# Finer runs in the edge sort of a graph-attention kernel: rows of 32 with runs of 8, masks in descending order, a layer norm shared by two engines

## The chip, the cores and the metric

The kernel runs on one core of one Trainium2 chip. The metric is the device time of one execution in microseconds (us). Every kernel is executed several times, and profiled once by the hardware profiler. A 0.3% difference, about 7 us, is what a measurement of this kernel can tell from none.

## The reference

The input is a graph with N = 6250 nodes of width D = 256 and E = 100000 edges (`src`, `dst`). Cut to what matters:

```python
xn = _layernorm(x)
x = x + gnn(xn, W_w, W_b, a_w, a_b, src, dst) + mix(xn)
x = x + ffn(_layernorm(x))
# gnn: Wh = xn @ W_w + W_b; e = leaky(f_dst[dst] + f_src[src] + a_b)
#      softmax of e over the edges of each src node, then the weighted sum of Wh[dst], relu
# mix: linear attention (phi(q), phi(k), 8 heads) @ Wo + bo, residual, layer norm 1 (l1g, l1b),
#      relu(. @ W1 + b1) @ W2 + b2, residual, layer norm 2
# ffn: mixture of 6 experts, two per node, three layers each
```

## The kernel before, in words

The program is a sequence of blocks with a barrier between them; inside a block five engines run hand-ordered instruction lists that meet at semaphores.

**Block 1** (L450 to L1243) makes the node table `wh_table`, sorts the edges by their source block, and does the attention half of `mix`. There are NT = 50 node blocks of R = 125 rows. The 100000 edges lie on 128 partitions as KC = 28 chunks of W = 28 columns each.

*The first pass* (until about 300 us) counts: for each block ScalarE makes a mask, VectorE scans it. From the counts VectorE works out (L681 to L698) where each run, that is the edges of one chunk and partition that belong to one block, begins. Runs are padded to LO = 64 places.

*The second pass* (L755 to L766, 50 steps b = 0 to 49) gives each edge its place: a mask "block is b" lets `copy_predicated` (L764) write the base of block b's run into `bpos`. For even b the mask comes from ScalarE in two instructions, Abs (L935) and Relu (L939); for odd b VectorE makes it itself with `is_equal` (L761).

*The address part* (L771 to L864) turns places into a row `hih` and a column `loh` of a small matrix of HI = 106 rows by LO = 64 columns per chunk, and works out where each row goes in DRAM (`dest`, L793 to L797: a compare-and-multiply and a reduction over 1400 elements).

*The compaction* (L893 to L909 on VectorE, 28 chunks k) places the edges of one chunk into their matrix by one-hot matmuls. Per chunk VectorE makes the one-hot rows (`first_half`, L873), the one-hot columns (`low_half`, L876) and two payloads (`payload`, L879 and L880); TensorE multiplies them (`compact`, L1206, 28 matmuls); ScalarE copies a half (L1068); `join` (L888) puts the two halves together in `stage`, of which there are three. GpSimd then writes the matrix to DRAM in one indirect DMA per chunk (L532): one address per row, 64 elements behind it. It waits for the write of the chunk before to have landed (L531), because a later chunk's run overwrites the padding of an earlier one; `join` waits for the write three chunks back (L887). When all have landed, SP reads the sorted slots back (L482), they are transposed and become the index and row tables, and block 1 ends.

*The attention of `mix`* is threaded through all of this after the first pass: 25 chunks of 250 nodes, a new one every SLOT = 6 slots, each with steps at fixed slot offsets on PE, ACT and DVE (the four functions `attend`). A slot is one step of the second pass, then one of TAB_SLOTS places in the address part, then a quarter of a compaction chunk. The steps that matter here are `attend_sum` at offset 13 (DVE: residual, bias, `bn_stats`, `bn_aggr`), `root` at 14 (ACT), and `attend_norm` at 15, where VectorE applies layer norm 1 in two passes of two instructions (`norm_out`, L293 and L299). SP stores the result `x1` to DRAM (L471).

**Block 2** (L1305 to L1694) is the graph attention. GpSimd gathers the table rows of the edges, 812 indirect DMAs of 128 rows (L1330). The other engines go over NG = 251 groups of four tiles in a software pipeline (`together`, L100): a group is at `turn` at lag 1 and `fetch` at lag 3 on PE, at `total` at lag 6 (L1648) and at `gather_up` at lag 7 on DVE (L1438). The feed-forward half of `mix` is threaded in, one of the 25 chunks every PER = 10 slots: 250 slots, then TAIL = 8 slots in which the last groups drain. In slot 1 ScalarE copies the turned input `x1T` out of PSUM (`feed_in`, L1577). Layer norm 2 of a chunk (`feed_sum` L1446, bias, moments L1457, totals, centre L1470, scale, out L1485) is done by VectorE in slots 0 to 5 of the next ten.

**Blocks 3 and 4** route the nodes to experts (with indirect writes of 128 rows of 1056 bytes, L1839) and run the experts (with accumulating indirect writes of 128 rows of 1024 bytes, L2139). The diff does not touch them.

Of the kernel before, what the change touches and what calls it, by code (L numbers as in the profile page):

```python
# [14 lines left out]
I32 = mybir.dt.int32  # L15
# [38 lines left out]
SPARE = 940  # L54
SLOT, TAB_SLOTS = 6, 8
# [12 lines left out]
TAIL = NG - PER * NC + LAG  # L68
assert L == 2 ** 7 and TILES - GT >= MOST and NB - RING <= NG <= 2 * L and 3 <= TAIL <= PER and NT * R == N and NC * 2 == NT

# [57 lines left out]
def gps_kernel(nc, x, src, dst, gW, gWb, ga, gab, Wq, bq, Wk, bk, Wv, bv, Wo, bo, W1, b1, W2, b2,  # L128
# [6 lines left out]
    with ExitStack() as ctx:  # L135
# [60 lines left out]
        rs = take(2, 2)  # L196
        pair_rows = take.place[0]
# [49 lines left out]
        dest = take(KC).bitcast(I32)  # L247
        dsum, dcol = take(KC), take(KC)
        icol, i64 = take(1), take(1)
# [5 lines left out]
        prod = E_  # L255
# [11 lines left out]
        held_gpsimd = sem("held_gpsimd")  # L267

        def hold(eng):

            eng.sem_inc(held_gpsimd if eng is nc.gpsimd else held_vector, 1)

        def norm_in(dve, c, k, bias):

            mine = m_ln[k]
            dve.wait_ge(mine, at(c, 4, 1))
            nc.vector.tensor_tensor(y1[0:R, k, :, :], y1[0:R, k, :, :], bias[0:R, :].unsqueeze(1).to_broadcast([R, 2, D]), ALU.add).then_inc(mine, 1)
            dve.wait_ge(mine, at(c, 4, 2))
            for r in range(2):
                last_s = nc.vector.bn_stats(stats[0:R, k, r, :], y1[0:R, k, r, :])  # L280
            last_s.then_inc(mine, 1)
            dve.wait_ge(mine, at(c, 4, 3))
            hold(dve)
            for r in range(2):
                last_s = nc.vector.bn_aggr(mv[0:R, k, r, :], stats[0:R, k, r, :])
            last_s.then_inc(m_va[k], 1)

        def norm_out(dve, c, k, dst_of, gam, bet):

            mine = m_ln[k]  # L290
            dve.wait_ge(m_va[k], at(c, 1, 1))
            for r in range(2):
                last_s = nc.vector.scalar_tensor_tensor(y1[0:R, k, r, :], y1[0:R, k, r, :], mv[0:R, k, r, 0:1], gam[0:R, :],  # L293
                                                ALU.subtract, ALU.mult)
            last_s.then_inc(mine, 1)
            dve.wait_ge(mine, at(c, 4, 4))
# [2044 lines left out]
```

## Time and profile before

| | us |
|---|---|
| runs, unprofiled | 2337.33, 2339.25, 2344.64 |
| their median | 2339.25 |
| the profiled execution, own time | 2334.28 |
| its span, first to last instruction | 2332.6 |
| second pass | 327.3 to 436.4 |
| address part | 436.4 to 475 |
| compaction, to the last write's landing | 475 to 741 |
| block 2 | from about 749 to 1820.5 |
| blocks 3 and 4 | 1820.5 to 2332.6 |

In the rows below times are us from the span's start unless marked ns, and L12 is line 12 of the kernel. PE is TensorE's matmul, PEld its weight load, DVE VectorE, ACT ScalarE, POOL GpSimd, SP SyncE. A busy PE is modelled and not PE at its peak; spans on POOL are rough, and end when the instruction is done, not when its data has landed. "Releaser" is what an engine's idle time ended with.

### The profile page before, as it was taken

How to read it: one execution, taken by the hardware profiler on the slowest of the kernel's cores; microseconds unless marked ns; L12 is line 12 of the kernel's file. 1: busy time of each engine (PE TensorE's matmuls, PEld its weight loads, DVE VectorE, ACT ScalarE, POOL GpSimd, SP SyncE). 2: the span in 40 equal slices, each digit the busy share in tenths (PEclk: the TensorE clock that was granted, in tenths of full speed). 3: DMA queues.
4: the chain of work that ended last, by engine and by line, in shares of the span. 5: the costliest groups of instructions: out<-in, count | busy, mean ns of one | idle time of the engine just before them, and what ended most of it. 6: DMA issues, size and time to landing. Idle time of an engine off the chain costs nothing. (4 is left out here: it accounts for less than half of the span.)

```text
span 2332.6 us, 50389 instructions
## 1 busy us (share of the span) xinstructions
PE 1929.0 (83%) x10277; PEld 1565.8 (67%) x10277; DVE 1757.9 (75%) x5456; ACT 1446.1 (62%) x4447; POOL 1106.9 (47%) x1090
## 2 busy tenths in 40 slices
PE   2888856678884799999999999999999563699996
PEld 1444435467773587787877877778787463588885
DVE  7877769989995688888888888888888652254553
ACT  4666647423330588888988889898898661233332
POOL 1000000001113777777777767777775267255554
PEclk9999978779995799999999999999999765799999
DMA  4200000011111444444444434444443543255553
GB/s 139 65 24 28 27 7 19 14 55 22 22 22 37 118 118 122 118 123 118 122 119 118 123 109 113 118 116 123 115 121 86 163 162 133 63 89 96 92 95 56
DMA packets 115204, 205.88 MB, mean 88 GB/s; under 512 B 27026, under 2 KB 69387, under 8 KB 114907
## 3 DMA queue, kind: packets, MB, share of 16 engines
q0 software_dynamic: 61648, 135.33, 24.2%
q1 hardware_dynamic: 48601, 59.88, 8.5%
q10 hardware_dynamic: 4658, 7.46, 1.1%
q8 instruction: 96, 1.57, 0.3%
q14 instruction: 201, 1.65, 0.2%
HBM read 146.67 MB, written 50.02 MB: 84 GB/s over the span
## 5 line engine op out<-in xcount | busy, mean ns | idle before, releaser
L1330 POOL DMA_INDIRECT area<-wh_table,area x812 | 782.5, 964 | 269.5 <-issue 241.7
L1648 PE MATMUL bank<-area 128*126 x2008 | 495.9, 389 | 35.1 <-ACT area L1564 15.7
L1648 PEld LDWEIGHTS bank<-area 128*126 128x126 f32 x2008 | 357.6, 188 | 110.3 <-issue 59.5
L1363 DVE TENSOR_SCALAR area<-iota_row,area 128x126 f32<-128x126 f32 x1004 | 359.7, 366 | 22.2 <-ACT area L1524 18.2
L1557 ACT ACTIVATE area<-iota_row,area 128x126 f32<-128x126 f32 x753 | 292.2, 389 | 0.4 <-ACT area L1564 0.3
L2139 POOL DMA_INDIRECT out_dram<-area x108 | 169.5, 1570 | 165.2 <-DVE area L2200 148.5
L1571 ACT ACTIVATE area<-area 128x126 f32<-128x126 f32 x753 | 243.1, 386 | 0.5
L527 POOL IOTA acc_mem<- 50x812 f32 x1 | 0.8, 807 | 450.0 <-DVE area L797 450.0
L1438 DVE SCALAR_TENSOR_TENSOR acc_mem<-acc_mem,area,bank 125x258 f32 x251 | 120.4, 480 | 110.6 <-PE bank L1636 97.6
L1510 ACT ACTIVATE area<-bank 125x512 bf16<-125x512 f32 x251 | 149.3, 595 | 85.9 <-DVE area L1377 83.6
L1668 PE MATMUL bank<-area 128*128 128x250 f32 x800 | 190.4, 381 | 5.9 <-ACT area L1577 3.1
L1624 PE MATMUL bank<-ident,area 128*126 128x128 f32 x1004 | 161.3, 284 | 35.5 <-DVE area L1363 34.7
L1679 PE MATMUL bank<-area 128*125 128x256 f32 x800 | 189.0, 379 | 0.0
L1668 PEld LDWEIGHTS bank<-area 128*128 128x128 f32 x800 | 154.3, 193 | 26.2 <-ACT area L1577 3.5
L1377 DVE TENSOR_REDUCE area<-bank 125x1 f32<-125x512 f32 x251 | 171.3, 682 | 0.0
L1679 PEld LDWEIGHTS bank<-area 128*125 128x125 f32 x800 | 150.1, 188 | 22.9
L532 POOL DMA_INDIRECT sorted_slots<-area x28 | 45.9, 1641 | 234.2 <-DVE area L888 213.3
L2200 DVE SCALAR_TENSOR_TENSOR area<-bank,area 128x256 f32<-128x256 f32 x108 | 47.3, 479 | 143.4 <-DMA out_dram<-area 78.0
L1624 PEld LDWEIGHTS bank<-ident,area 128*126 128x126 f32 x1004 | 106.3, 141 | 40.4 <-DVE area L1363 39.7
L2232 ACT ACTIVATE area<-bank,area 128x256 f32<-128x256 f32 x108 | 45.3, 471 | 141.6 <-issue 133.6
L1839 POOL DMA_INDIRECT moe_rows<-area x100 | 99.3, 993 | 66.6 <-ACT area L1989 36.7
L1206 PE MATMUL bank<-area 128*128 128x128 f16 x784 | 104.6, 298 | 7.5 <-DVE area L888 7.5
(409 smaller groups left out, 4188.8 us busy)
## 6 DMA issues: line engine op xcount, KB each, us to landing
area<-moe_rows SPq DMA_DIRECT2D x54, 264.0 KB, 2.7
area<-wh_table,area POOLq DMA_INDIRECT x812
area<-area SPq DMA_DIRECT2D x18, 388.5 KB
wh_table<-area SPq DMA_DIRECT2D x50, 126.5 KB
xn<-in_x_dram SPq DMA_DIRECT2D x25, 250.0 KB
x_rows<-area SPq DMA_DIRECT2D x25, 250.0 KB
area<-x_rows ACTq DMA_DIRECT2D x24, 250.0 KB
area<-in_L_ffn_expert_w_dram SPq DMA_DIRECT2D x3, 1536.0 KB, 11.8
```

The source lines that it names most:

```text
L1330: g.indirect_dma_start(out=gath[:, (i + GT) % RS, :], out_offset=None, in_=table, in_offset=bass.IndirectOffsetOnAxis(ap=idx_tab[:, i:i + ...
L1363: ins = V.tensor_scalar(xm[:, b, t, :], iota_row[:, :], rowl[:, j % 10, t:t + 1], fetched(j, D)[:, t:t + 1], ALU.is_equal, ALU.mult)
L1377: V.tensor_reduce(gmax[0:R, b:b + 1], bank[XT[j % 2]][0:R, :], AX.X, ALU.max).then_inc(d_m, 1)
L1438: V.scalar_tensor_tensor(row, row, alpha[0:R, j % 5:j % 5 + 1], bank[US[b]][0:R, 0:WROW], ALU.mult, ALU.add).then_inc(d_acc, 1)
L1510: A.activation(hot[0:R, b, :], bank[XT[j % 2]][0:R, :], ACT.Sign).then_inc(a_hot, 1)
L1557: last = A.activation(dist[:, t, :], iota_row[:, :], ACT.Abs, bias=rowl[:, j % 10, t:t + 1], scale=-1.0)
L1571: last = A.activation(sm[:, b, t, :], dist[:, t, :], ACT.Exp, bias=e3[:, b, t:t + 1], scale=-1.0e12)
L1624: last = T.transpose(bank[XT[j % 2]][0:RW, t * L:(t + 1) * L], xm[:, b, t, :], ident[:, :])
L1648: last = T.matmul(bank[US[b]][0:RW, 0:WROW], sm[:, b, t, :], gath[:, bass.ds(place + t, 1), 0:WROW].rearrange("p a w -> p (a w)"), start=( ...
L1668: last = T.matmul(bank[HB[p % 2]][:, i * CH:(i + 1) * CH], w_1[:, k, f * 128:(f + 1) * 128], x1T[:, k, :], start=(k == 0), stop=(k == 1))
L1679: last = T.matmul(bank[AB][0:R, r * D:(r + 1) * D], hT[:, f, r * R:(r + 1) * R], w_2[:, f, :], start=(f == 0), stop=(f == 7))
L2139: g.indirect_dma_start(out=out, out_offset=bass.IndirectOffsetOnAxis(ap=rowi[:, j % RB6, s, MW - 2:MW - 1], axis=0), in_=yo[:, j % 3, s, : ...
```

## The change

- Rows of the compaction matrix get LO = 32 columns in place of 64, and runs are padded to RUN = 8 places in place of 64. HI goes from 106 to 123 rows of the matrix, and the write uses all 128 partitions. A row now holds RL = 4 runs, and each goes to an address of its own.
- The indirect write of a chunk becomes four, one for each run of a row: 128 addresses with 8 elements (32 bytes) each. They are issued without a wait between them; the wait for the chunk before stays. The addresses are worked out four times, once for each run of a row.
- Less padding makes 788 tiles in place of 812, and 245 groups (NG) in place of 251. TAIL becomes 6.
- The second pass goes downward, b = 49 to 0. Its mask is "block is at most b", one Relu on ScalarE for every b; what is written wrongly is overwritten later. VectorE's own masks and the Abs are gone. There are four mask buffers in turn.
- Layer norm 1: VectorE works out minus mean times root on a [125, 2] tile (offset 15), ScalarE applies scale and shift in two activations (`normal`, offset 16), VectorE multiplies by the gain in one instruction (offset 17). The shift `l1b` is added by ScalarE when it copies `x1T` out of PSUM (two instructions in place of one), and once to `bias_2`. TAB_SLOTS becomes 10.

The diff, cut to its core:

```diff
-LO, LO_BITS = 64, 6
-HI = (L * W + NT * (LO - 1)) // LO + 1
+LO, LO_BITS = 32, 5
+RUN, RUN_BITS = 8, 3
+RL = LO // RUN
+HI = (L * W + NT * (RUN - 1)) // LO + 1
-MOST = (E + NT * (LO - 1) + L - 1) // L
+MOST = (E + NT * (RUN - 1) + L - 1) // L
-SLOT, TAB_SLOTS = 6, 8
+SLOT, TAB_SLOTS = 6, 10
-TAIL = NG - PER * NC + LAG
+TAIL = max(6, NG - PER * NC + LAG)
...
                     if k > 0:
-                        g.wait_ge(sent_runs, 16 * k)
-                    g.indirect_dma_start(out=slots.rearrange("(a b) -> a b", b=1),
-                                         out_offset=bass.IndirectOffsetOnAxis(ap=dest[0:HI, k:k + 1], axis=0),
-                                         in_=stage[0:HI, k % 3, :], in_offset=None).then_inc(sent_runs, 16)
+                        g.wait_ge(sent_runs, 16 * RL * k)
+                    for j in range(RL):
+                        g.indirect_dma_start(out=slots.rearrange("(a b) -> a b", b=1),
+                                             out_offset=bass.IndirectOffsetOnAxis(ap=dest[:, j, k:k + 1], axis=0),
+                                             in_=stage[:, k % 3, j * RUN:(j + 1) * RUN], in_offset=None).then_inc(sent_runs, 16)
...
+                V.tensor_tensor(bias_2, bias_2, be1, ALU.add)
...
+                def attend_gain(c, j):
+                    dve.wait_ge(m_n, at(c, 1, 1))
+                    V.tensor_tensor(x1[0:R, j, :, :], x1[0:R, j, :, :], g1[0:R, :].unsqueeze(1).to_broadcast([R, 2, D]), ALU.mult).then_inc(m_x1, 1)
...
-                def attend_norm(c, j):
-                    if at(c) >= 2:
-                        dve.wait_ge(rows_moved[j], 16 * SG + at(c, 8, -8 * j))
-                    norm_out(dve, c, 0, x1[0:R, j, :, :], g1, be1).then_inc(m_x1, 1)
+                def attend_norm(c):
...
+                    V.scalar_tensor_tensor(nmu[0:R, :], mv[0:R, 0, :, 0], -1.0, rs[0:R, 0, :], ALU.mult, ALU.mult).then_inc(m_va[0], 1)
...
-                for b in range(NT):
-                    if b % 2 == 0:
-                        dve.wait_ge(mask_ready, NT + b // 2 + 1)
-                        m = masks[(b // 2) % 2]
-                    else:
-                        m = masks[2 + (b // 2) % 2]
-                        step(V.tensor_scalar(m, blk, float(b), None, ALU.is_equal))
-                    if b > 0:
-                        dve.wait_ge(placed, NT + b)
+                for i in range(NT):
+                    b, m = NT - 1 - i, masks[i % 4]
+                    dve.wait_ge(mask_ready, NT + i + 1)
+                    if i > 0:
+                        dve.wait_ge(placed, NT + i)
...
-                step(V.scalar_tensor_tensor(E_[:, 0:KC, :], pin, icol, delta[:, 0:KC, :], ALU.is_le, ALU.mult))
-                step(V.tensor_reduce(dsum, E_[:, 0:KC, :], AX.X, ALU.add))
-                attend(NT + 6)
-                step(V.tensor_tensor(dcol, dsum, D_[:, :, 0:1].rearrange("p k b -> p (k b)"), ALU.add))
-                V.tensor_scalar(dest, dcol, i64, None, ALU.add).then_inc(dest_ready, 1)
+                for i in range(RL):
+                    step(V.scalar_tensor_tensor(over_runs, pin, icol[:, i:i + 1], delta[:, 0:KC, :], ALU.is_le, ALU.mult))
+                    step(V.tensor_reduce(dsum[:, i, :], over_runs, AX.X, ALU.add))
+                    attend(NT + 6 + i)
+                    step(V.tensor_tensor(dcol[:, i, :], dsum[:, i, :], first, ALU.add))
+                    last_d = V.tensor_scalar(dest[:, i, :], dcol[:, i, :], irun[:, i:i + 1], None, ALU.add)
...
+                def normal(c, j):
+                    act.wait_ge(m_va[0], at(c, 2, 2))
+                    if at(c) >= 2:
+                        act.wait_ge(rows_moved[j], 16 * SG + at(c, 8, -8 * j))
+                    for r in range(2):
+                        last = A.activation(x1[0:R, j, r, :], y1[0:R, 0, r, :], ACT.Identity, bias=nmu[0:R, r:r + 1], scale=rs[0:R, 0, r:r + 1])
+                    last.then_inc(m_n, 1)
...
+                def at_most(i):
+
+                    b = NT - 1 - i
+                    act.wait_ge(placed, NT + max(0, i - 3))
+                    A.activation(masks[i % 4], blk, ACT.Relu, bias=iota_blk[:, b + 1:b + 2], scale=-1.0).then_inc(mask_ready, 1)
...
-                    A.copy(x1T, bank[TB][:, 0:2 * CH].rearrange("p (k n) -> p k n", k=2)).then_inc(m_tc1, 1)
+                    for k in range(2):
+                        last = A.activation(x1T[:, k, :], bank[TB][:, k * CH:(k + 1) * CH], ACT.Identity, bias=be1_col[:, k:k + 1])
+                    last.then_inc(m_tc1, 1)
```

## Rows read from the trace of the kernel before

**Rows 1.** The head of the page.
```profile
span 2332.6 us, 50389 instructions
```

**Rows 2.** Busy time per stage: PE, PEld, DVE, ACT, POOL, PEclk, DMA share, GB/s.
```profile
327.30:436.40 109.10, 72.60 (x308) 60.11 (x308) 98.81 (x170) 79.74 (x134) 0.00 (x0) 0.76 0.05 15
436.40:475.00 38.60, 19.45 (x68) 13.49 (x68) 35.70 (x97) 9.07 (x22) 0.81 (x1) 0.64 0.05 14
503.40:715.00 211.60, 182.22 (x1219) 160.52 (x1218) 196.94 (x328) 67.15 (x178) 36.02 (x23) 0.96 0.14 33
757.70:1798.20 1040.50, 969.66 (x5632) 811.75 (x5633) 888.92 (x3481) 899.04 (x3226) 776.51 (x806) 0.99 0.43 118
1798.20:1820.50 22.30, 15.85 (x85) 11.51 (x83) 16.03 (x58) 17.20 (x62) 0.00 (x0) 1.00 0.01 1
```

**Rows 3.** Groups by line, second pass (327.3 to 436.4): count, busy us, mean ns, idle.
```profile
L935 ACT ACTIVATE acc_mem<-acc_mem,iota_blk 128x784 f32<-128x784 f32 x25 | 23.7, 949 | 14.4 <-issue 14.4
...
L761 DVE TENSOR_SCALAR acc_mem<-acc_mem 128x784 f32<-128x784 f32 x25 | 13.6, 544 | 0.0
...
L1006 ACT ACTIVATE area<-xn,area 125x256 f32<-125x256 f32 x18 | 9.7, 589 | 0.0
```

**Rows 4.** Timeline of DVE in the address part: start, duration.
```profile
452.94 1.64 DVE L793 SCALAR_TENSOR_TENSOR area<-area 128x1400 f32<-128x1400 f32 x1
454.62 1.61 DVE L794 TENSOR_REDUCE area<-area 128x28 f32<-128x1400 f32 x1
```

**Rows 5.** Groups by line, compaction from 503.4 to 715.
```profile
L873 DVE TENSOR_TENSOR area<-acc_mem 128x2968 f16<-128x2968 f16 x24 | 40.8, 1701 | 6.3 <-PE bank L1206 5.5
...
L876 DVE TENSOR_TENSOR area<-acc_mem,area 128x1792 f16<-128x1792 f16 x23 | 24.6, 1068 | 0.0
...
L299 DVE SCALAR_TENSOR_TENSOR area<-area 125x256 f32<-125x256 f32 x32 | 14.1, 482 | 0.6
...
L277 DVE TENSOR_TENSOR area<-area 125x512 f32<-125x512 f32 x15 | 10.4, 692 | 0.5
```

**Rows 6.** Timeline of POOL at the end of the compaction.
```profile
726.81 1.54 POOL L532 DMA_INDIRECT sorted_slots<-area  x1 [2.97 <-DMA sorted_slots<-area]
731.70 1.55 POOL L532 DMA_INDIRECT sorted_slots<-area  x1 [3.35 <-DMA sorted_slots<-area]
```

**Rows 7.** Line L532, the indirect write of the compaction: ns min/median/max, landing.
```profile
L532 POOL DMA_INDIRECT sorted_slots<-area x28: 1543/1547/3729, 503.8 to 736.6; - x28
...
DMA to landing us min/median/max: 3.6/4.1/8.9
```

**Rows 8.** Line L1839, the indirect write of block 3.
```profile
L1839 POOL DMA_INDIRECT moe_rows<-area x100: 965/970/1507, 1849.3 to 1988.6; - x100
...
DMA to landing us min/median/max: 2.4/2.6/4.7
```

**Rows 9.** Line L2139, the accumulating indirect write of block 4.
```profile
L2139 POOL DMA_INDIRECT out_dram<-area x108: 1542/1551/1783, 2024.4 to 2322.8; - x108
```

**Rows 10.** Timeline of POOL in block 3: two writes in a row.
```profile
1855.11 0.97 POOL L1839 DMA_INDIRECT moe_rows<-area  x1 [0.30 <-issue]
1856.38 0.97 POOL L1839 DMA_INDIRECT moe_rows<-area  x1 [0.30 <-issue]
```

**Rows 11.** DMA view, 721 to 727, which holds the packets of one indirect write.
```profile
DMA packets 80, 0.03 MB, mean 5 GB/s; under 512 B 72, under 2 KB 74, under 8 KB 80
...
sorted_slots<-area POOLq DMA_INDIRECT x2, 3.8
```

**Rows 12.** Timeline of DVE in the tail of block 2.
```profile
1801.91 0.69 DVE L1446 TENSOR_TENSOR area<-bank,area 125x512 f32<-125x512 f32 x1
...
1808.77 0.75 DVE L1457 BATCH_NORM_STATS2 area<-area 125x6 f32<-125x256 f32 x2
...
1811.45 0.87 DVE L1470 SCALAR_TENSOR_TENSOR area<-area 125x256 f32<-125x256 f32 x2
...
1820.02 0.48 DVE L1438 SCALAR_TENSOR_TENSOR acc_mem<-acc_mem,area,bank 125x258 f32 x1 [1.60 <-PE bank L1648]
```

**Rows 13.** Line L1577, the copy of x1T: ns min/median/max.
```profile
L1577 ACT COPY area<-bank x25: 548/552/556, 766.9 to 1765.5; 128x500 f32<-128x500 f32 x25
...
  PE bank L1668: 3.1, 1
```

More of the change, by code:

```diff
@@ L196, in gps_kernel @@
         rs = take(2, 2)
+        nmu = take(2)
+        be1_col = take(2)
         pair_rows = take.place[0]
@@ L266, in gps_kernel @@
         held_vector = sem("held_vector")
-        held_gpsimd = sem("held_gpsimd")
         def hold(eng):
[L271 to L278, printed above, removed]
+            eng.sem_inc(held_vector, 1)
@@ L283, in norm_in @@
             hold(dve)
             for r in range(2):
[L285 to L296, printed above, removed]
-            dve.wait_ge(m_rs[k], at(c, 1, 1))
-            for r in range(2):
-                last_s = nc.vector.scalar_tensor_tensor(dst_of[:, r, :], y1[0:R, k, r, :], rs[0:R, k, r:r + 1], bet[0:R, :],
-                                                ALU.mult, ALU.add)
-            return last_s
+                last_s = nc.vector.bn_aggr(mv[0:R, 0, r, :], stats[0:R, 0, r, :])
@@ L778, in _ @@
                 cnt = Sv[:, KC, :]
-                step(V.tensor_scalar(ntf, cnt, float(LO - 1), None, ALU.add))
+                step(V.tensor_scalar(ntf, cnt, float(RUN - 1), None, ALU.add))
                 attend(NT + 1)
@@ L800, in _ @@
                 V.tensor_copy(int50, tend)
-                step(V.tensor_scalar(end50, tend, float(L - LO), None, ALU.add))
+                step(V.tensor_scalar(end50, tend, float(L - RUN), None, ALU.add))
                 V.tensor_scalar(int50, int50, 7, None, ALU.logical_shift_right)
@@ L1002, in prepare @@
                     m = at(c) % 3
-                    wait(act, m_ln[0], at(c, 4, -11))
+                    wait(act, m_ln[0], at(c, 3, -8))
                     for r in range(2):
@@ L1031, in inverses @@
                     A.copy(rec_row[0:R, :, :, :], rec8[0:R, :, :].unsqueeze(3).to_broadcast([R, 2, 8, HD])).then_inc(m_inv, 1)
+                def normal(c, j):
[5 more added lines that the diff above has]
+                    last.then_inc(m_n, 1)
                 def attend(slot):
+                    c = chunk_at(slot, 16)
+                    if c is not None:
+                        normal(c, at(c) % 2)
                     c = chunk_at(slot, 14)
@@ L1067, in _ @@
                             act.wait_ge(staged, k - 3)
[L1068 removed]
+                        A.copy(half[:, k % 2, :], bank[KV + k % 2][:, LO:2 * LO]).then_inc(halved, 1)
                     for i in range(4):
@@ L1173, in o @@
                     pe.wait_ge(m_att, at(c, 1, 1))
-                    wait(pe, m_ln[0], at(c, 4, -3))
+                    wait(pe, m_ln[0], at(c, 3, -2))
                     for r in range(2):
```

82 lines of the change are left out of this document (47 added, 35 removed).

## The prediction, made before the changed kernel ran

> **What bounds the kernel now.** I first read the span [rows 1] and the chain of waits. The chain covers only the last 300 us (blocks 3 and 4, which are not touched), since a barrier ends every block; so each stage has to be read by itself. The view of busy time per stage does that [rows 2]. In the second pass DVE is busy 98.8 of 109.1 us; in the address part 35.7 of 38.6; in the compaction 196.9 of 211.6. All three are bound by DVE. In block 2 PE is busy 970 of 1040 us: PE bounds it, and the gathers of POOL (777 us) do not. The reader is to see that fewer gathers are worth nothing by themselves; fewer groups are, because each is PE work.
>
> The compaction I then read by line [rows 5] and on POOL [rows 6, 7]. The 23 chunks of the window take 211.6 / 23 = 9.2 us each. POOL writes once per chunk and otherwise waits for DVE's `join`. Only at the end, when no attention is left, does the write's own loop show: start to start 731.70 - 726.81 = 4.89 us, in which the next write waits for the landing [rows 6]. The landing there is 3.8 us after the issue [rows 11], so 1.09 us pass between landing and the next start. Half of those 9.2 us is slack, and the change fills it with three more writes.
>
> **The change part by part** (bounds in brackets).
>
> *Second pass.* DVE loses 25 masks, 13.6 us [rows 3], and per norm four instructions of 0.48 us against one of 0.69 [rows 5] and a tiny one, for which I take 0.1: 1.13 us. Six norms fall here: 6.8 us. DVE is then busy 98.8 - 13.6 - 6.8 = 78.4 us. ACT swaps 25 Abs and 25 Relu for 50 Relu of the same shape (the Abs, like the Relu, take 0.95 us [rows 3]), which is no change, and gains 12 activations that I price as L1006, 0.589 us: 79.7 + 7.1 = 86.8. So ACT takes over as the bound. If it reaches the share that DVE has now (0.91) the stage takes 95.8 us; as ACT also waits for PE and DVE in turn, I take 99: **-10** [0 to -22].
>
> *Address part.* Three more rounds of 1.64 + 1.61 us [rows 4] and two small operations: +10. Two norms, each 1.13 shorter, fall here: -2. DVE is bound, so all of it counts: **+8** [7 to 11]. The addition to `bias_2` is a 256-element instruction, under 0.5 us, within this.
>
> *Compaction.* DVE: from 2968 to 1792 elements L873 and L876 differ by 0.633 us, 0.538 ns per element [rows 5]. The one-hot rows grow to 28 x 123 = 3444 elements: 1.96 us, +0.26. Three instructions shrink to 896 elements: 0.59 us each, -0.48 three times, which makes -1.19 with rounding. Two thirds of an attention chunk pass per chunk, so the norm saves 0.75. DVE's loop becomes 9.2 - 1.19 - 0.75 = 7.3 us. PE's busy time is 182.2 / 23 = 7.9 us per chunk now [rows 2], and its compaction matmuls move half as many columns, so it is no more than that.
>
> POOL: four issues and one landing per chunk. The price of an issue is the open question. The write of 106 rows takes 1.55 us [rows 7]; the write of 128 rows of 1056 bytes takes 0.97 and lands 2.6 us after its issue, not 4.1 [rows 8]; the accumulating one of 128 rows takes 1.55 again [rows 9]. I take 0.97. The reason is the packets of one present write: 80 of them, six with 2 to 8 KB though no row has more than 256 bytes, and 72 under 512 bytes [rows 11]. That is a write cut unevenly, with many small pieces beside the data; 106 is an awkward number of rows, and 128, which the cheap write has, is not. With a pitch of 1.27 us [rows 10], POOL's loop is 3 x 1.27 + 2.6 + 1.09 = 7.5 us. By the Trainium skill (DMA: Bandwidth & Descriptors, "Why a DMA increments its semaphore by 16 and not by 1") a DMA runs on as many engines, up to 16, as divide its outermost dimension: 106 rows on 2, 128 on 16. By that rule the landing shortens as I assume, and without it (4.1 us less the shorter issue) the sum below would be -24 in place of -42; the view names no engines, so no row here shows it.
>
> Three loops of 7.3, 7.5 and at most 7.9 us that hand to each other through three buffers, beside the stores of `x1`, don't reach the best of them: I take 7.8 per chunk. From the first to the last write's start there are now 736.6 - 503.8 = 232.8 us [rows 7]; then 27 x 7.8 + 3.8 = 214.4, and the last landing is 1.2 us shorter: **-20** [-34 to +55, the ends being 7.3 us, and 10.5 as worked out under the rivals]. The three chunks that lead in before the first write save 1.19 each: **-4** [0 to -6].
>
> *Block 2.* Six groups go, but not six slots of 4.1 us: the feed-forward holds 250 slots. In the slots from 246 on, PE lacks the `turn` of groups that aren't there, half a us each: -2. The tail took 22.3 us [rows 2], with `total` and `gather_up` up to 1820.5 [rows 12]. After it holds one group and the last norm 2, whose seven steps on DVE are 0.69 + 0.69 + 0.75 + 0.25 + 0.87 + 0.88 + 0.68 us (L1446, L1457 and L1470 in [rows 12]; the bias add is like the first, the last two like L1470 and L1446), with the root on ACT between: about 7. So **-17** [-14 to -19]. The 24 gathers that go are hidden behind PE. `feed_in` becomes two activations: at most 0.55 us more 25 times, and PE waited for it once, 3.1 us in all [rows 13]: **+1** [0 to 14].
>
> *Nothing* for the extra load and for the smaller read-back of the slots: the load lies under the first pass, the read-back still is one short transfer.
>
> Sum: -10 + 8 - 4 - 20 - 17 + 1 = -42 us. The profiled execution took 2334.3 us, 1.7 over its span, so it would take 2292; the median of the runs is 5 us above it, so the forecast for the median is **2297 us**.
>
> **The rivals.**
> 1. *The writes become the bound* (ends slower). If an issue of 128 addresses with 32 bytes costs what the present write costs, a chunk needs 3 x 1.86 (1.55 and the 0.3 between issues [rows 7, 10]) + 4.89 = 10.5 us, longer than 9.2 now. First to last start: 27 x 10.5 + 5.6 = 288, +55; the other terms stay: +33, or 2372 us. With the short landing (1.6 us after the issue's end) it is 9.8 per chunk and 2354. It decides from about 9.3 us per chunk on. For it: the destination is still addressed by single elements, and the accumulating write of 128 rows takes 1.55 too. Against it: the accumulating one has a reason of its own, and the plain write of 128 rows is cheap. Chance 0.16.
> 2. *DVE holds POOL up* (slower as well). One present issue took 3.73 us in place of 1.55 [rows 7]. If one of the four in every chunk met that, 2.2 to 2.8 us come on top of 7.5: about 10.3 per chunk, 2367 us. The Trainium skill (SBUF — State Buffer, "SBUF: two separate sides") says that VectorE and GpSimd exclude each other on a shared port pair, and that GpSimd then cannot write its descriptors. The trace bears it out little: the median of the 28 writes, most of them issued while DVE works, is 4 ns over the minimum. Chance 0.04.
> 3. *The landing stays long.* Issue 0.97, but landing 2.55 us after its end as now: 8.4 per chunk, compaction -2, sum -24, 2315 us. For it: rows of 32 bytes may land no sooner than rows of 256. Chance 0.12.
> 4. *Nothing couples.* ACT never idle in the second pass (-22) and 7.3 us per chunk (-33): 2267 us. Against it: DVE itself idles 7 to 9% of these stages now [rows 2]. Chance 0.05.
>
> **How the numbers follow.** The forecast has 0.63, and by itself spans 2280 to 2312. The range goes from 2272, short of rival 4, to 2354, the lower end of rival 1: outside are most of rival 4 and most of rivals 1 and 2, under 0.2 in all. A measurement tells 0.3%, 7 us, from no change. Faster than 2332: the forecast, rival 4 and half of rival 3, 0.74. Within: 0.06, from rival 3's longer landings and rival 1's shorter issues. Slower: rivals 1 and 2, 0.20.
>
> **What would show it.** In the changed profile L532's successor has 112 issues; a median near 0.97 us and start to start 1.27 within a chunk bears out the main step, 1.55 and 1.86 is rival 1, a median far over the minimum rival 2, a landing over 4 us rival 3. POOL's idle time should still end partly with DVE's `join`; if it ends with landings alone, POOL is the bound. The second pass should last near 99 us with ACT the busiest, the address part near 47, block 2's tail about 7. I am wrong if the compaction's chunks take over 9.3 us, or if `normal` on ACT makes DVE wait so that the second pass keeps its 109 us.

## The result, and the profile after

The changed kernel takes 2322.61 us (median of 14 runs, 2308.94 to 2328.54), the one before 2337.68 us beside it: a ratio of 0.9934, 95% interval 0.9919 to 0.9948. It is faster by 15 us. The forecast was 2297 us, 41 us less.

The profiled execution of after is the lowest of its 14 runs (2308.94 us). A second profiled one, of a later run of the same kernel (after_again below, span 2316.2), is nearer the median, and the account by stages uses it. The stages are cut at the first and last placing instruction of the second pass, the first write's start, the last write's end, the readers of the slots, and the first write of block 3.

```
stage                          before  after again  change  forecast
first pass                      329.3     331.8      +2.5       0
second pass                     103.9      93.3     -10.6     -10
address part and lead-in         70.6      76.4      +5.8      +4
compaction, first to last write 234.3     237.6      +3.3     -20
read-back of the slots            9.2       8.2      -1.0       0
block 2                        1102.0    1086.2     -15.8     -16
blocks 3 and 4                  483.3     482.7      -0.6       0
span                           2332.6    2316.2     -16.4     -42
```

Three of the four stages that the forecast touches come out within 2 us of it. One failed, by 23 us: the compaction did not get shorter at all. First, the windows of after that answer to [rows 2], in its first profile (same columns: stretch and length, busy time of PE, PEld, DVE, ACT and POOL, granted clock, DMA share, GB/s). The third is the compaction from the first write's start to that of the 23rd chunk, 22 chunks; the last the tail of block 2.

```profile
326.90:422.00 95.10, 64.84 (x308) 54.40 (x308) 80.96 (x135) 82.27 (x146) 0.00 (x0) 0.84 0.06 17
422.00:472.20 50.20, 21.92 (x76) 15.45 (x76) 45.45 (x106) 11.01 (x26) 0.79 (x1) 0.63 0.04 11
495.84:691.43 195.59, 157.04 (x1216) 136.39 (x1214) 155.25 (x294) 80.21 (x205) 111.54 (x88) 0.90 0.12 34
757.70:1789.27 1031.57, 967.21 (x5605) 808.97 (x5606) 881.00 (x3444) 899.44 (x3236) 745.48 (x778) 0.99 0.42 115
1789.27:1796.00 6.73, 1.71 (x8) 1.13 (x6) 5.23 (x12) 0.50 (x2) 0.00 (x0) 0.85 0.00 0
```

In the compaction DVE is busy 155.25 / 22 = 7.1 us per chunk and PE 7.1, as the prediction worked out (7.3 and at most 7.9). But a chunk takes 195.59 / 22 = 8.9 us. Neither engine is full any more: each is busy 80% of the time, where DVE had 93% [rows 2]. What they wait for stands in the view of groups by line of the same window; [rows 5] has the like of L870 (there L873) and [rows 7] of L522.

```profile
L522 POOL DMA_INDIRECT sorted_slots<-area x88 | 111.5, 1268 | 123.0 <-DMA sorted_slots<-area 62.0 <-DVE area L885 40.9 <-issue 20.1
...
L870 DVE TENSOR_TENSOR area<-acc_mem 128x3444 f16<-128x3444 f16 x24 | 46.9, 1952 | 24.4 <-PE bank L1219 24.3
...
L1190 PE MATMUL bank<-area 128*125 128x256 f32 x120 | 39.0, 482 | 12.6 <-DVE area L714 12.5
L1163 PE MATMUL bank<-area 128*128 128x250 f32 x104 | 29.0, 427 | 16.8 <-ACT area L1009 16.8
```

Two things are to be seen. POOL is full: 111.5 us of issues, 62.0 of waiting for a landing and 20.1 between issues make 193.6 of 195.6 us (the 40.9 us for DVE lie ahead of the first write). And DVE waits 24.3 us for L1219, the compaction's matmuls, before it may make the next high one-hot rows; in the kernel before that wait was 5.5 us [rows 5].

POOL's loop taken apart, by its timeline. Undisturbed, at the end of the stage, it is shorter than the 7.5 us that I had worked out:

```profile
721.53 0.97 POOL L522 DMA_INDIRECT sorted_slots<-area  x1 [1.92 <-DMA sorted_slots<-area]
722.80 0.97 POOL L522 DMA_INDIRECT sorted_slots<-area  x1 [0.30 <-issue]
724.08 0.97 POOL L522 DMA_INDIRECT sorted_slots<-area  x1 [0.30 <-issue]
725.35 0.97 POOL L522 DMA_INDIRECT sorted_slots<-area  x1 [0.30 <-issue]
728.23 0.97 POOL L522 DMA_INDIRECT sorted_slots<-area  x1 [1.91 <-DMA sorted_slots<-area]
```

From 721.53 to 728.23 are 6.70 us: four issues of 0.97, and 1.9 us until the last has landed. Beside working engines the same loop reads like this:

```profile
568.48 0.97 POOL L522 DMA_INDIRECT sorted_slots<-area  x1 [4.06 <-DMA sorted_slots<-area]
569.75 2.36 POOL L522 DMA_INDIRECT sorted_slots<-area  x1 [0.30 <-issue]
572.41 1.28 POOL L522 DMA_INDIRECT sorted_slots<-area  x1 [0.30 <-issue]
574.00 1.05 POOL L522 DMA_INDIRECT sorted_slots<-area  x1 [0.30 <-issue]
579.10 1.45 POOL L522 DMA_INDIRECT sorted_slots<-area  x1 [4.05 <-DMA sorted_slots<-area]
```

That is 10.6 us. Two terms grew. One issue took 2.36 us, and the timelines of DVE and SP in the same microseconds show beside what:

```profile
569.31 1.95 DVE L870 TENSOR_TENSOR area<-acc_mem 128x3444 f16<-128x3444 f16 x1 [0.49 <-PE bank L1219]
```

```profile
574.23 0.25 SPq L460 DMA_DIRECT2D x_rows<-area  x1
```

L870 ends at 571.26, the issue at 572.11, 0.85 us later: it began while L870 ran and was held until that was over. The wait for the landing, 4.05 us in place of 1.9, lies beside a store of `x1` (250 KB) that SP issued at 574.23. In the 22 chunks six such waits last 4.03 to 4.08 us, and each time SP had issued a store 0.8 us before the chunk's last issue ended.

### The profile page after: what moved, and what is told of

Its sections match the earlier page's. It is cut to its first block and busy times, and to the rows that moved or that the text cites. A ratio compares the mean times of both kernels' runs of the same rounds, so it can differ in the third digit from the quotient of the medians.

```text
span 2307.2 us, 49748 instructions
## 1 busy us (share of the span) xinstructions
PE 1871.2 (81%) x10181; PEld 1515.7 (66%) x10181; DVE 1684.1 (73%) x5316; ACT 1450.3 (63%) x4450; POOL 1170.9 (51%) x1150
## 5 line engine op out<-in xcount | busy, mean ns | idle before, releaser
L1343 POOL DMA_INDIRECT area<-wh_table,area x788 | 755.5, 959 | 262.5 <-issue 236.0
L1663 PE MATMUL bank<-area 128*126 x1960 | 482.8, 389 | 29.0 <-ACT area L1584 15.6
L1663 PEld LDWEIGHTS bank<-area 128*126 128x126 f32 x1960 | 348.8, 188 | 101.6 <-issue 53.2
L1376 DVE TENSOR_SCALAR area<-iota_row,area 128x126 f32<-128x126 f32 x980 | 352.5, 370 | 23.6 <-ACT area L1537 14.6
L1570 ACT ACTIVATE area<-iota_row,area 128x126 f32<-128x126 f32 x735 | 285.4, 389 | 0.1
L1584 ACT ACTIVATE area<-area 128x126 f32<-128x126 f32 x735 | 237.3, 387 | 0.4
L522 POOL DMA_INDIRECT sorted_slots<-area x112 | 138.1, 1233 | 140.0 <-DMA sorted_slots<-area 65.8
L1694 PE MATMUL bank<-area 128*125 128x256 f32 x800 | 188.9, 379 | 0.0
L1694 PEld LDWEIGHTS bank<-area 128*125 128x125 f32 x800 | 149.8, 187 | 23.2
L2290 PE MATMUL bank<-area 128*128 128x256 f32 x432 | 105.8, 389 | 2.8 <-ACT area L2239 1.7
```

The source lines that it names most:

```text
L1343: g.indirect_dma_start(out=gath[:, (i + GT) % RS, :], out_offset=None, in_=table, in_offset=bass.IndirectOffsetOnAxis(ap=idx_tab[:, i:i + ...
L1376: ins = V.tensor_scalar(xm[:, b, t, :], iota_row[:, :], rowl[:, j % 10, t:t + 1], fetched(j, D)[:, t:t + 1], ALU.is_equal, ALU.mult)
L1570: last = A.activation(dist[:, t, :], iota_row[:, :], ACT.Abs, bias=rowl[:, j % 10, t:t + 1], scale=-1.0)
L1584: last = A.activation(sm[:, b, t, :], dist[:, t, :], ACT.Exp, bias=e3[:, b, t:t + 1], scale=-1.0e12)
L1663: last = T.matmul(bank[US[b]][0:RW, 0:WROW], sm[:, b, t, :], gath[:, bass.ds(place + t, 1), 0:WROW].rearrange("p a w -> p (a w)"), start=( ...
L1694: last = T.matmul(bank[AB][0:R, r * D:(r + 1) * D], hT[:, f, r * R:(r + 1) * R], w_2[:, f, :], start=(f == 0), stop=(f == 7))
```

## The experiments

All labels are kernels made from the changed one unless the text says otherwise. "Per chunk" is the time from the first write's start to that of the 23rd chunk, over 22; it and the last column come from one profile of each kernel. The last three rows, described at the end, leave the compaction as it is in after: without any edit to it, a chunk takes 8.89 to 9.33 us. A smaller difference in that column shows nothing by itself.

```
kernel             us       ratio [95%]               per chunk  DVE waits for the matmuls
before             2337.7   1                            9.11       5.5
after              2322.6   0.9934 [0.9919, 0.9948]      8.89      24.3
two_tables         2312.6   0.9902 [0.9880, 0.9924]      9.11      30.3
stores_timed       2321.7   0.9939 [0.9922, 0.9956]      8.82      26.0
hot_rows_split     2322.6   0.9942 [0.9922, 0.9962]      8.98      24.6
two_writes         2314.6   0.9906 [0.9883, 0.9929]      9.08      23.8
early_alone        2313.8   0.9892 [0.9867, 0.9918]      8.72       0
timed_early        2301.1   0.9836 [0.9803, 0.9868]      8.11       0
timed_early_split  2293.8   0.9808 [0.9783, 0.9832]      7.90       0
two_tables_early   2280.0   0.9766 [0.9750, 0.9782]      7.57       0
two_tables_fill    2308.7   0.9888 [0.9872, 0.9905]      8.86      27.6
two_writes_early   2290.5   0.9806 [0.9789, 0.9822]      8.06       0
before_early       2335.9   0.9980 [0.9966, 0.9995]      9.01       0
before_128         2330.7   0.9972 [0.9956, 0.9987]      9.04       5.0
after_again        2319.8   0.9920 [0.9898, 0.9943]      9.03      25.1
groups_251         2330.7   0.9959 [0.9942, 0.9976]      9.33      29.3
old_masks          2321.2   0.9924 [0.9898, 0.9950]      8.90      25.6
```

### POOL's loop made shorter in four ways

My first theory was that POOL's loop had become the bound. Each of four kernels takes another piece of it away.

*two_tables*, the wait for the landing:

```diff
-  if k > 0:
-      g.wait_ge(sent_runs, 16 * RL * k)
+  mine, to = ((sent_runs, slots), (sent_odd, slots_b))[k % 2]
+  if k > 1:
+      g.wait_ge(mine, 16 * RL * (k // 2))
```

> The odd chunks write into a second tensor with a semaphore of its own, so a chunk's writes wait for the landing of the chunk but one before; half of the edges are then missing from the slots that are read back. Theory (POOL's loop of four issues and a landing is the bound of the compaction, about 6.0 + 2.5 = 8.5 us per chunk): without the wait for the landing POOL needs about 6.3 us, DVE's 7.3 to 7.9 per chunk takes over, and the 236 us from the first to the last write become 197 to 213; the kernel 2284 to 2300 us against 2323. Rival (DVE and PE need the 8.5 us themselves, POOL only looks full): POOL idles for DVE's join instead, first to last write stays 232 to 240, 2318 to 2328 us.

*stores_timed*, the meeting of stores and landings:

```diff
   sp.wait_ge(m_x1, at(c, 1, 1))
+  wait(sp, sent_runs, 16 * RL * min(KC, (SLOT * at(c) + 17 - NT - TAB_SLOTS) // 4 - 2))
   sp.dma_start(x1_rows[...], x1[...]).then_inc(rows_moved[j], 16)
```

> SP holds each store of x1 until the chunk before the present one has landed. Theory (a store's 250 KB hold up the landing): the 7 landings of the first 23 that a store now stretches to about 4.05 us fall to 1.9 to 2.6, 13.5 us less waiting in all; POOL being the bound, 8 to 14 us of it are gained, 2308 to 2315 us. Rival (landings are long for another reason, or POOL is not the bound): landings stay as long as they are, or get shorter with the time unchanged, 2318 to 2328 us.

*hot_rows_split*, the longest of the instructions beside which an issue is held:

```diff
-  V.tensor_tensor(oh_hi[k % 2][:, :, 0:HI, :], each(hih, k, HI), ...)
+  for a in range(0, WO, 2):
+      b = min(WO, a + 2)
+      V.tensor_tensor(oh_hi[k % 2][:, a:b, 0:HI, :], each(hih, k, HI)[:, a:b], ...)
```

> The one-hot rows of the high half (1.95 us) are made by four instructions of about 0.5 us. Theory (an issue that begins while an instruction with two SBUF inputs runs on DVE is held until that one ends, plus 0.85 us): no issue lasts over about 1.5 us any more; the 19 issues held by L870, some 20 us in all, lose about 15 to 18 of them; DVE pays 0.2 us per chunk; 5 to 15 us gained, 2308 to 2318 us. Rival (DVE holds POOL through a whole run of instructions, or the holds are covered): issues stay up to 2.6 us, the time rises by DVE's 3 to 6 us, 2323 to 2330 us.

*two_writes*, two of the four writes:

```diff
-LO, LO_BITS = 32, 5
-RUN, RUN_BITS = 8, 3
+LO, LO_BITS = 64, 6
+RUN, RUN_BITS = 32, 5
-SPARE = 0
+SPARE = 940
-SLOT, TAB_SLOTS = 6, 10
+SLOT, TAB_SLOTS = 6, 8
```

> Runs padded to 32 places and chunks compacted in rows of 64, so two writes per chunk and 81 high rows; two slots of attention fewer beside the address part. Theory (POOL's loop is the bound with four writes): with two it needs 1.27 + 0.97 + 2.5 and some 0.6 of holds, 5.3 us, so DVE bounds again; from 9.2 us per chunk before the change the norm takes 0.75 and 81 rows in place of 106 another 0.38: 8.1 per chunk, 219 us from first to last write (236 now); the address part loses two rounds, 7 us; the lead-in gains 2; about 2301 us. Rival (the bound is PE or the coupling of the engines, which before the change had the same 128 columns per matmul): 8.6 to 9.0 per chunk, 232 to 243 us, 2316 to 2327 us.

Every edit did to POOL what it was meant to do, and none shortened the chunk beyond that spread. In stores_timed the view of waits puts only 10.5 us on landings (62.0 in after), but the windows give 194.11 / 22 = 8.8 us:

```profile
POOL sorted_slots L523 <- DVE area L886: 90.0, 18, 40.3
...
DVE area L871 <- PE bank L1220: 26.0, 19, 3.5
...
POOL sorted_slots L523 <- DMA sorted_slots<-area: 10.5, 4, 4.7
```

POOL now waits for DVE's `join` (49.7 us without the 40.3 ahead of the first write), and DVE for PE. In hot_rows_split no issue takes over 1.44 us (2.59 in after), which bears out how an issue is held, and the time is that of after (its line and that of after stand below). In two_tables, where POOL waits for no landing at all, a chunk takes 9.11 us. Its 10 us and the 8 us of two_writes in the whole kernel are not won in these 22 chunks. What the profiles show of them lies behind, where no attention is left (from the 23rd chunk to the 28th 29.4 and 25.5 us, 36.8 in after and 34.1 in after_again); two_writes also lacks two rounds of the address part, and its block 2 is 8 to 10 us longer, with three groups more (248). So the theory fell as it stood: POOL is full in after, but right behind it lies a second loop of the same length, that of DVE and PE.

```profile
L522 POOL DMA_INDIRECT sorted_slots<-area x112: 963/972/1444, 503.1 to 739.7; - x112
```

```profile
L522 POOL DMA_INDIRECT sorted_slots<-area x112: 967/972/2588, 495.8 to 732.1; - x112
```

### The second loop

The timeline of two_tables shows it. First the matmuls of `q` (L1168) at one iteration, then at another, with what follows:

```profile
605.50 1.95 PE L1168 MATMUL bank<-area 128*128 128x250 f32 x8 [1.20 <-ACT area L1014]
...
617.03 3.34 PE L1168 MATMUL bank<-area 128*128 128x250 f32 x8 [1.36 <-ACT area L1014]
...
620.16 0.63 PE L1224 MATMUL bank<-area 128*128 128x64 f16 x7
...
620.83 1.95 DVE L875 TENSOR_TENSOR area<-acc_mem 128x3444 f16<-128x3444 f16 x1 [3.69 <-PE bank L1224]
```

DVE stands for 3.69 us until the last seven matmuls of a chunk (L1224) are done, for only then are the rows of that buffer free. Those seven are done late because PE works in program order: they stand behind `q`, which waited 1.36 us for ACT and then ran 3.34 us. A theory of hand-over follows: DVE can't start a chunk until PE has been through a whole iteration, attention included, and PE's attention waits in turn for DVE and ACT. It was tested by one edit, made to several of the kernels: PE's 28 matmuls of a chunk in the first two of an iteration's parts and ahead of the attention there:

```diff
+  if 1 <= k <= KC and i < 2:
+      compact(k - 1, 2 * i)
+      compact(k - 1, 2 * i + 1)
   attend(NT + TAB_SLOTS + 4 * k + i)
-  if 1 <= k <= KC:
-      compact(k - 1, i)
```

(The two matmuls of `gmap_done` in the iteration k = 1 go ahead of them.)

> As two_tables, and PE does the 28 matmuls of a chunk in the first two of an iteration's four parts, each ahead of that part's attention, in place of seven behind each part. Half of the edges are missing from the slots, as there. Theory (with POOL out of the way the bound is the hand-over between PE and DVE: DVE may make the next one-hot rows only when PE has finished a whole iteration, attention included): DVE's wait for the compaction's matmuls falls from 30 us to under 12 in the window of 23 chunks, a chunk takes 8.0 to 8.4 us in place of 9.1, and the kernel 15 to 25 us less than two_tables: 2288 to 2298 us. Rival (the waits inside attention, PE at its lower clock among them, set the pace): the waits only move to attend_sum and to the matmuls of o and q, 8.9 to 9.3 us per chunk, 2308 to 2317 us.

> Two writes per chunk (rows of 64, runs padded to 32) and PE's matmuls in the first two parts of an iteration. Theory of the hand-over: DVE's wait for the compaction's matmuls (24 us in the window of 23 chunks of two_writes) falls under 10, a chunk takes 8.1 to 8.4 us in place of 9.1, close to DVE's busy 7.6; 2292 to 2300 us against 2315. Rival (PE bounds: 8.1 us busy per chunk and its own waits for attention): 8.8 to 9.1 us, 2307 to 2316 us.

> The changed kernel with x1's stores held back as in stores_timed and PE's matmuls in the first two parts of an iteration; four writes per chunk, full output. Theory of the hand-over: POOL's own loop, 6.0 us of issues and 1.9 to 2.2 of landing, bounds what is left: 8.0 to 8.4 us per chunk in place of 8.8, 2302 to 2313 us against 2322. Rival: no change from stores_timed, 2318 to 2326 us.

> The changed kernel with one edit: PE's matmuls of a chunk in the first two parts of an iteration. Theory (two loops of nearly equal length lie one behind the other, POOL's of issues and landing with 8.9 us per chunk and the hand-over of PE and DVE with 8.8 to 9.1): POOL's remains, eased only where a store no longer meets a landing: 8.4 to 8.9 us per chunk, 2311 to 2323 us against 2323. Rival (the hand-over alone was the bound, POOL only looked full): 8.0 to 8.2 us per chunk as in timed_early, 2299 to 2306 us.

> The kernel before the change with PE's matmuls of a chunk in the first two parts of an iteration. Theory (before the change DVE was the bound, and waited for the compaction's matmuls 5.5 us only in the window of 23 chunks): 8.7 to 9.0 us per chunk in place of 9.1, 3 to 8 us gained, 2329 to 2334 us. Rival (the hand-over set the pace before the change as well): 8.1 to 8.4 us per chunk, 15 to 25 us gained, 2312 to 2322 us.

The group of the high one-hot rows, in two_tables_early and then in two_writes_early, over their 22 chunks:

```profile
L875 DVE TENSOR_TENSOR area<-acc_mem 128x3444 f16<-128x3444 f16 x23 | 44.6, 1938 | 0.0
```

```profile
L870 DVE TENSOR_TENSOR area<-acc_mem 128x2268 f16<-128x2268 f16 x22 | 29.2, 1326 | 0.2 <-issue 0.2
```

The wait is gone, and so are 33 us against two_tables and 24 against two_writes (medians), both more than the theory had asked, and 1.5 and 1.0 us per chunk, well over the spread. The whole window of two_writes_early:

```profile
497.91:675.17 177.26, 170.31 (x1191) 156.53 (x1190) 165.37 (x282) 81.46 (x203) 60.69 (x45) 0.99 0.13 39
```

PE and DVE are busy 96% and 93% of it: here a bound by work is back. On the changed kernel with its four writes the same edit alone brings 9 us, and together with the timed stores 22, for POOL's loop is then what is left (in timed_early it waits for a landing 20 times in these 22 chunks, 42.9 us in all, and 18 of the 20 waits are 1.9 us long). So in after two loops of nearly the same length hold each chunk, and taking one away leaves the other: 8.89 us per chunk as it is, 8.82 and 8.72 with one of the two edits, which is within the spread, 8.11 with both.

On the kernel before, the edit brings 3 us by medians and 9.01 us per chunk, both just short of what was expected: DVE was the bound there, and the hand-over covered.

### The holds, where POOL is the bound

> timed_early with the high one-hot rows made by four instructions of about 0.5 us. POOL's loop is the bound in timed_early (it waits for the landing 20 times of 23). Theory of the holds (an issue waits until the DVE instruction with two SBUF inputs that was running has ended, plus 0.85 us): the mean of a chunk's four issues falls from 6.0 us to 5.0 to 5.4, a chunk from 8.1 to 7.4 to 7.7, and the kernel by 8 to 18 us, 2283 to 2293 us against 2301. Rival (DVE holds POOL as long as it runs any such instructions in a row): issues stay at 5.8 to 6.2 us, 2299 to 2306 us.

It has the edits of hot_rows_split and timed_early. Its L522 is L523:

```profile
L523 POOL DMA_INDIRECT sorted_slots<-area x112: 967/973/1444, 496.9 to 709.5; - x112
```

A chunk's four issues fall from a mean of 6.01 us (first start to last end) to 5.37, as expected. The kernel falls by 7 us, short of what was expected, and the intervals of the two ratios overlap. A chunk takes 7.9 us where 7.4 to 7.7 were expected, since DVE's `join` is waited for again (81.6 us, 42.2 of them ahead of the first write). The same edit was worth nothing in hot_rows_split.

### The granted clock

PE's granted clock is 0.97 in the kernel before from 503.78 to 704.21, 0.90 in after, 0.86 in two_tables. The windows of before and of two_tables:

```profile
503.78:704.21 200.43, 175.52 (x1172) 154.72 (x1171) 187.40 (x311) 66.14 (x173) 34.47 (x22) 0.97 0.15 34
```

```profile
500.48:700.80 200.32, 162.85 (x1189) 139.96 (x1187) 150.76 (x288) 79.11 (x203) 111.95 (x89) 0.86 0.12 32
```

In the example above it is 1.00 around the first `q` and 0.56 in the second, near the lower of the two levels (1.2 GHz). Ahead of the second PE had stood 1.36 us for ACT; but ahead of the first it had stood 1.20 us, so that one wait doesn't tell the two apart:

```profile
603.00:607.45 4.45, 3.25 (x29) 2.82 (x28) 3.74 (x10) 2.67 (x8) 1.03 (x2) 1.00 0.02 2
617.03:620.37 3.34, 3.34 (x12) 2.58 (x13) 0.10 (x2) 0.62 (x1) 2.43 (x3) 0.56 0.03 2
```

*two_tables_fill* gives PE more to do, on zeros:

```diff
   if part == 3:
       last.then_inc(gathered_up, 1)
+  else:
+      for c in range(5):
+          T.matmul(bank[KV + k % 2][:, 0:(L - HI) * WI], oh_hi[k % 2][:, c // WI, :, c % WI],
+                   oh_hi[k % 2][:, 0, HI:L, :], start=False, stop=False)
```

> As two_tables, and behind each of the first three parts of a chunk PE runs five more matmuls that add zeros, some 1.2 us per chunk in all. Theory (the compaction is longer because PE's granted clock falls, 0.86 in two_tables against 0.97 before the change): PE waits less, the clock stays at 0.95 or more, and a chunk takes 8.3 to 8.8 us in place of 9.1 in spite of more work: 2297 to 2306 us. Rival (the hand-over between PE and DVE sets the pace and the clock only follows it): the added matmuls lie on the path, 9.2 to 10.0 us per chunk, 2314 to 2332 us.

```profile
502.30:697.17 194.87, 163.10 (x1526) 146.56 (x1526) 150.72 (x288) 79.16 (x203) 106.24 (x88) 0.91 0.12 34
```

PE runs 1526 instructions in place of 1189, its busy time is the same (163.10 and 162.85 us), the clock 0.91 in place of 0.86, and a chunk is 0.25 us shorter. That is under the least the theory asked (0.3 us per chunk; 4 us in all where 6 to 15 were expected) and within the spread of 8.89 to 9.33 us, and the intervals of the two ratios overlap. So PE had room for more work without a longer chunk, against the rival; that a higher clock shortens the chunk is not shown. (groups_251, the longest of the unedited compactions, has the lowest clock of the four, 0.87 where the others have 0.90; which of the two brings the other stays open.) What the runs do show is the order of PE's work, with 1.5 and 1.0 us per chunk in two_tables_early and two_writes_early.

### The price of a write

*before_128* is the kernel before with one change to its write:

```diff
-  out_offset=bass.IndirectOffsetOnAxis(ap=dest[0:HI, k:k + 1], axis=0),
-  in_=stage[0:HI, k % 3, :], in_offset=None).then_inc(sent_runs, 16)
+  out_offset=bass.IndirectOffsetOnAxis(ap=dest[:, k:k + 1], axis=0),
+  in_=stage[:, k % 3, :], in_offset=None).then_inc(sent_runs, 16)
```

(and `join` and the copy of `half` over 128 rows).

> The kernel before the change, its one write per chunk taken over all 128 rows of 256 bytes in place of 106; the added rows hold zeros and go behind the slots. Theory (the number of addresses, 106 or 128, sets the price): the issue's median falls from 1.55 to 0.97 us and the landing comes 1.9 to 2.1 us after its end in place of 2.55 to 3.3; the time stays, 2332 to 2342 us, for POOL has slack. Rival (32 bytes in place of 256 made the new write cheap): issue still 1.5 to 1.9 us.

The page of the line, and the packets of one write at the end (the DMA view from 725.9 to 729.2):

```profile
L532 POOL DMA_INDIRECT sorted_slots<-area x28: 971/971/2182, 507.8 to 732.5; - x28
...
DMA to landing us min/median/max: 2.4/2.7/5.0
```

```profile
DMA packets 32, 0.03 MB, mean 10 GB/s; under 512 B 16, under 2 KB 16, under 8 KB 32
```

More rows, and the issue is 0.97 us in place of 1.55, the landing 2.7 after the issue in place of 4.1 [rows 7], the packets 32 in place of 80 [rows 11]. So the number of rows made the old write dear, not their 256 bytes. That the time would stay was a miss: it falls by 8 us (0.9972), in the last chunks, where the kernel before waits for landings [rows 6]. From the 23rd write to the 28th it takes 25.8 us, 32.4 in the kernel before.

### The other terms

*groups_251* adds five empty groups:

```diff
-NG = (MOST + NT - 1 + NT * (GT - 1)) // GT
+NG = (MOST + NT - 1 + NT * (GT - 1)) // GT + 5
```

> The changed kernel with NG raised by five, to the 251 groups of before; the five added ones hold no edges. Theory (a group costs a slot of block 2 even at its end, 1040 us / 254 slots = 4 us or a little less): block 2 gets back 15 to 20 us, 2337 to 2343 us against 2323. Rival (as the prediction had it: the groups themselves are worth about 2 us, the shorter norm after the last one the rest): 2 to 6 us, 2324 to 2329 us.

That makes 250 groups, not the 251 of the label and of the recorded text, and a TAIL of 7. Median 2330.7 us (0.9959, 0.9942 to 0.9976), 8 us over after. Block 2, from the readers of the slots to block 3, takes 1092.6 us in place of 1083.4 and 1086.2 in the two profiles of after: 6 to 9 us for five groups, less than the theory and more than the rival. The traces show where they lie. From the end of the last feed-forward matmul (L1694) to block 2's last instruction pass 17.5 us here, 6.8 in both profiles of after and 22.2 in the kernel before, and to block 3's first write 46.0, 35.1 and 51.0. What comes ahead of that matmul takes 1047 to 1051 us in all four. So the groups cost what they take to drain behind the last feed-forward chunk, 10.8 us for five, and the 16 us that the change brings in block 2 all lie there. (This execution's compaction was 7 us longer than that of after_again, with no edit there; I leave that open.)

*old_masks* puts back the loop over the blocks of the second pass and ACT's two-step masks (the lines that the diff removes there).

> The changed kernel with the masks of the second pass as before: upward, every other mask made by DVE in 0.54 us, the others by ACT in two steps. Theory (the second pass is bound by DVE and ACT alike now, 81 and 82 of 95 us): DVE gets 13.6 us more, 95 us busy, and the pass lasts 102 to 106 us; 8 to 11 us more, 2330 to 2334 us. Rival (the shorter norm alone gave the 14 us): the pass stays under 98 us, 2321 to 2326 us.

The second pass takes 101.7 us (93.3 and 91.8 in after's two profiles), 8 to 10 us more, DVE busy 91.1 of it:

```profile
328.60:430.30 101.70, 71.60 (x302) 59.76 (x303) 91.05 (x153) 83.91 (x144) 0.00 (x0) 0.74 0.05 16
```

So the masks carry most of the second pass' gain. The whole kernel shows none of it: 2321.2 us (0.9924, 0.9898 to 0.9950). In this execution the first pass was 3 us shorter and block 2 again 3 us shorter than in after_again. What takes the stage's 8 us back in the median of four runs is not settled.

*after_again* is the changed kernel unchanged.

> The changed kernel once more, for a second profile. Theory (the spread of its time lies in the stages where the granted clock moves between its levels, first pass, second pass and compaction, and not in block 2): the median is 2318 to 2327 us, and of the difference in span to the first profile at least 7 in 10 lies ahead of block 2. Rival (block 2 or blocks 3 and 4 vary): the difference lies behind 745 us.

Median 2319.8 us (0.9920, 0.9898 to 0.9943), span of the profile 2316.2, 9.0 over the first. Of that, 6.3 us lie ahead of block 2 (4.0 of them in the first pass, 1.6 in the second), 2.8 in block 2: 7 in 10, as the theory had it by a hair.

## Why the prediction was wrong in its size

The sign was right, and the time lies in the range; the size was not. It said 41 us less, 15 were measured, and one step makes the difference, the compaction.

- **Second pass** (-10): right, -10.6 in after_again, with ACT the busiest as forecast (82.27 and DVE 80.96 of 95.10 us).
- **Address part and lead-in** (+8 and -4): right, +5.8 together.
- **Block 2** (-17 and +1): right, -15.8, and by its main term: the tail fell from 22.2 to 6.8 us, as worked out. The 2 us for the missing `turn` and the 1 us for `feed_in` are too small to be seen in the rest of the block (1048 to 1051 us in the three profiles of before and after).
- **Price of an issue** (0.97 us): right, and for the reason argued, the number of rows. By the Trainium skill (DMA: Bandwidth & Descriptors, "Why a DMA increments its semaphore by 16 and not by 1") a DMA uses the largest number of engines, up to 16, that divides the outermost dimension of both its sides, which makes 16 for 128 rows and 2 for 106. before_128 agrees, with a landing of 2.7 us in place of 4.1, though no view names the engines.
- **Compaction** (-20): this is the step that failed. It said that three loops of 7.3, 7.5 and at most 7.9 us, handing to each other, would give 7.8 us per chunk. DVE's and PE's busy times came out as worked out, 7.1 each; 8.9 us per chunk were measured. Two things were left out. I had worked out POOL's loop from undisturbed rows (it is 6.7 us there, 8.9 beside DVE and the stores). And I had taken busy times for loops: PE's 7.9 us held none of its waits for attention, and the wait of DVE for the compaction's matmuls, which [rows 5] shows with 5.5 us, was never carried forward. With these waits and holds taken out together, in timed_early_split, a chunk takes 7.90 us, near the forecast's 7.8. When DVE lost 1.5 us of work per chunk (196.94 / 23 [rows 2] to 155.25 / 22), that wait rose to 24.3 us and PE's clock fell from 0.97 to 0.90; how much of the 8.9 us the clock makes stays open. The prediction's own sign for a bound on POOL, idle time that ends with landings alone, came true (62.0 us, and DVE only ahead of the first write), and misled: two_tables, without those waits, has no shorter chunk.

Of the rivals, the second (DVE holds POOL up, 0.04) was nearest in mechanism: the median of the issue, 0.97 us, does not show it, but the mean does, 1.23 us over the 112 writes (138.1 us), and 42 of them take over 1.1 us. It adds about 1.2 us to a chunk's four issues (6.0 where four undisturbed take 4.8), less than the 2.2 to 2.8 it was priced at. I had dismissed it since the median of the 28 old writes was 4 ns over the minimum. Only two of those were held at all: 13 of the 28 began beside DVE instructions with an input in PSUM (L723, L728), and none of the 13 took over 1.55 us; the added issues begin anywhere in DVE's work. By the Trainium skill (SBUF — State Buffer, "SBUF: two separate sides") VectorE and GpSimd exclude each other on a shared port pair, a VectorE instruction with two SBUF inputs only against a GpSimd one that reads SBUF, and whichever starts first has it for its whole instruction. The runs agree (2.59 us at most, 1.44 with the rows split). The third (landing stays long, 8.4 us per chunk) came nearest in time (2315 us) but not in cause: the landing is short, 1.9 us, unless a store crosses it. Rival 4's own terms (-22, +8, -4, -33, -17 and +1) give 2272 us and not 2267; nothing else hangs on that.

The changed kernel is not at its best: with PE's matmuls early and two writes of 32-place runs it takes 2290.5 us, 0.9806 of before, and with four writes, timed stores and split rows 2293.8.

## What to carry to other kernels

Where several engines hand to each other in program order, the bound after a cut is not the largest busy time: add to each engine's busy time the waits that come from its own program order, and look in the profile of before for a small wait of the engine whose work is cut (here 5.5 us), for it can grow (here to 24.3). Before an engine is given more instructions, ask beside which instructions the new ones will begin, and read their price there: a median over the old ones tells only of the places where those began. And when one edit at a suspected bound changes nothing, try it together with the next bound's: each alone gave at most 9 us here, both 22.

## What was not expected of the hardware

- An indirect write of 128 rows that begins while DVE runs an instruction with two SBUF inputs ends 0.84 to 0.85 us after that instruction (569.75 + 2.36 = 572.11; L870 ends at 571.26; so did all 19 that began beside L870 in after), unless its own 0.97 us of the undisturbed loop last longer.
- A landing of 1.9 us becomes 4.05 where a 250 KB store is under way, though a chunk's four writes are 4 x 128 rows of 32 bytes, 16 KB in all: six times of six in after's 22 chunks.
- More work for PE, on zeros (1526 instructions for 1189), left its busy time as it was (163.10 and 162.85 us), with the granted clock 0.91 for 0.86; the chunk was no longer for it.
